# A row-wise softmax inside a fused attention and mixture-of-experts kernel: the row maximum is subtracted on TensorE instead of VectorE

## The chip, the cores and the metric

One core of one Trainium2 chip. The metric is the device time in microseconds (us) of one execution; times "of the span" are counted from its first instruction. Engines go by their short names: PE (TensorE, matrix products), PEld (its weight loads), DVE (VectorE), ACT (ScalarE), POOL (GpSimd), SP (SyncE, here only loads and stores).

## The reference

Sixteen tiles of 128 tokens and 128 features. Each token is normalised and attends among its own 16 heads: 16 x 16 scores per token, softmax over the last axis, weighted sum of the values, output projection, residual. Then a second normalisation, a router that sends each token to 2 of 8 experts, and the experts.

```
scores = jnp.einsum('blhk,blgk->blhg', Q_, K_) / jnp.sqrt(jnp.float32(D_K))
attn = jax.nn.softmax(scores, axis=-1)
x = jnp.einsum('blhg,blgv->blhv', attn, V_)
...
x = x + _L0_xattn_ref(_layernorm(x, axis=-1), ctx_1024, ctx_1024, ...)
x = x + _L0_ffn_ref(_layernorm(x, axis=-1), L0_ffn_router_w, ...)
```

The part that matters is the softmax of attn: exponential of (score minus its row's maximum), over rows of 16, 16 rows per token, so a tile has 128 partitions x 256 numbers.

## The kernel before, in words

Everything is f32. The program is written by hand: each engine has its own stream, semaphores join them, and the order on each engine is the order in which `step(g, j)` issues. A step number is s = 2 + j + 4g; in step s an engine works on several tiles at once: `tile_at(g, j, lag)` is tile s − lag. Steps of the middle groups run in a hardware loop. One tile t goes through this:

- ACT writes xn (L564, two steps ahead), PE turns it (L763), ACT copies it out as xnT (L604), PE projects it (L743) into bank 1 or 5.
- Step t, DVE: the product qk of the projection with the context, 128 x 2048 (L1021). PE then makes the score sum in bank 2 or 3: one product L772 and eight L775 of 256 columns each, with the identity as one operand.
- Step t + 1, DVE: the negated maximum of each row (L1034, neg_max), then the subtraction from the scores in PSUM into the SBUF tile shifted (L1043). ACT takes the exponential of shifted (L572) and writes probs. POOL multiplies probs with the context, 128 x 2048 (L310, called here POOL's product; for tile 15 DVE does it itself). probs and that product are the two parts of sums_in.
- Step t + 2, DVE (`normalised`): sums sums_in into z0, in the spare columns of bank 3 or 2 (L990), reciprocal, z (L1009). PE turns z (L788), ACT copies zT (L612), PE makes the output product with bias and residual (L794 to L796), ACT copies it to x_sb (L617).
- Step t + 3, DVE: the statistics of the new row (L994, L1003).

Every four tiles are a group. At tile 0 DVE also computes the first normalisation's shifts of groups 1 to 3 (`shifts`, L929 and L931, 128 x 4 each). At step s = 7 + 4n (NORM) POOL has made the power for group n's second normalisation (L473), right ahead of its product of the next tile; DVE makes shift2 of it (L1062, 128 x 4), and then sums z0. At s = 8 + 4n (LOGITS) ACT copies the turned rows xn2T (L636, `turned`), PE makes the router product (L755), and DVE the top experts (L1074 to L1086). At s = 9 + 4n (PLACES) the places are worked out and POOL begins to scatter rows (L511). After the last group DVE takes its product of tile 15, early_table and the router's steps; then come the experts, bound by PE, 39 tiles at 2.79 us.

Of the kernel before, what the change touches and what calls it, by code (L numbers as in the profile page):

```python
# [16 lines left out]
ALU = mybir.AluOpType  # L17
# [6 lines left out]
P = 128  # L24
NT = 16
G = 4
NG = NT // G
H = 16
# [23 lines left out]
def xattn_moe_kernel(nc, x, ctx, Wq, bq, Wk, bk, Wv, bv, Wo, bo, router_w, wv, sv, w, s, w1, s1, out):  # L52
    stack = ExitStack()
    with stack:
        def sb(name, shape, dt=F32):
            return stack.enter_context(nc.sbuf_tensor(name, shape, dt))
# [58 lines left out]
        shifted = sb("shifted", [P, 2, H, H])  # L115
# [145 lines left out]
        def quarter_of(j, lag):  # L261

            return (AHEAD + j - lag) % G

        def q_bank(b):

            return bank[1 + 4 * b]

        def z0_of(b):

            return bank[3 - b][:, H * H:H * H + P + H]
# [78 lines left out]
        with nc.Block() as block:  # L350
# [181 lines left out]
            def _(act):  # L532
# [23 lines left out]
                def step(g, j):  # L556
# [9 lines left out]

                    if a := tile_at(g, j, 1):
                        t, b = a
                        act.wait_ge(s_shifted, t + 1)
                        if second_on(t):  # L570
                            act.wait_ge(z0_ready, t - 1)
                        nc.scalar.activation(probs[:, b, :, :], shifted[:, b, :, :], ACT.Exp).then_inc(p_ready, 1)  # L572
# [13 lines left out]
                    if isinstance(g, int) and group_at(g, j, LOGITS) == (NG - 2,):  # L586
                        turned(NG - 2)
# [105 lines left out]
            def _(pe):  # L693
# [33 lines left out]

                def value_turned():

                    pe.wait_ge(setup_dve, 4)  # L730
                    nc.tensor.transpose(bank[7][:, 0:P], o_projT[:, :], ident[:, :])
                    nc.tensor.transpose(bank[7][0:HD, P:2 * P], out_biasT[:, :], ident[:, :]).then_inc(setup_pe, 1)

                def step(g, j):

                    if a := tile_at(g, j, -1):
                        t, b = a
                        pe.wait_ge(xnT_ready, t + 1)
                        if second_on(t):
                            pe.wait_ge(qk_ready, t - 1)  # L740
                        elif t == 0:
                            pe.wait_ge(setup_dve, 3)
                        nc.tensor.matmul(q_bank(b)[:, 0:P], xnT[:, quarter_of(j, -1), :],  # L743
                                         q_proj[:, 0:HD, :].rearrange("p i h -> p (i h)"),
                                         start=True, stop=True).then_inc(q_psum, 1)
# [21 lines left out]
                    if a := tile_at(g, j, 0):  # L767
                        t, b = a
                        pe.wait_ge(qk_ready, t + 1)
                        if second_on(t):  # L770
                            pe.wait_ge(s_shifted, t - 1)
                        nc.tensor.matmul(bank[2 + b][:, 0:H * H], xnT[:, quarter_of(j, 0), :],  # L772
                                         q_proj[:, HD, :].unsqueeze(2).to_broadcast([P, H, H]), start=True, stop=False)
                        for i in range(HD):
                            mm = nc.tensor.matmul(bank[2 + b][:, 0:H * H], ident[:, :], qk[:, b, i, :],  # L775
                                                  start=False, stop=(i == HD - 1))
                        mm.then_inc(s_psum, 1)
                    if (a := group_at(g, j, LOGITS)) and not isinstance(g, int):
                        places(a[0])
# [120 lines left out]
            def _(dve):  # L900
# [76 lines left out]
                def step(g, j):  # L977
# [48 lines left out]
                    if a := tile_at(g, j, 1):  # L1026
# [6 lines left out]
                        scores = bank[2 + b][:, 0:H * H].rearrange("p (h g) -> p h g", h=H)  # L1033
                        v.tensor_reduce(neg_max[:, b, :], scores, AX_X, ALU.max, negate=True).then_inc(max_ready, 1)  # L1034
# [3 lines left out]
                    if a := tile_at(g, j, 1):  # L1038
                        t, b = a
                        dve.wait_ge(max_ready, t + 1)  # L1040
                        if second_on(t):
                            dve.wait_ge(p_ready, t - 1)
                        v.tensor_tensor(shifted[:, b, :, :], scores,  # L1043
                                        neg_max[:, b, :].unsqueeze(2).to_broadcast([P, H, H]), ALU.add).then_inc(s_shifted, 1)
# [238 lines left out]
```

## Time and profile before

| | us |
|---|---|
| median of 3 runs | 294.7 |
| lowest, highest | 293.94, 297.12 |
| the profiled execution | 297.16 |
| its span | 295.4 |

The page lists the busy time of each engine, the share of the span in 40 slices of 7.4 us, the granted clock of PE in tenths of full speed (2.4 GHz; 5 is 1.2 GHz), and the chain of work that ended last. The timeline lists instructions in order of their start: start, duration, engine, line, operation, tiles, and in brackets how long the engine was idle before and what ended that. Each f32 product is two records of PE, so x16 is eight products.

### The profile page before, as it was taken

What the parts mean: (1) busy time and instruction counts of PE and PEld (TensorE: products, weight loads), DVE (VectorE), ACT (ScalarE), POOL (GpSimd) and SP (SyncE); (2) the same over time, 40 slices, a digit from 0 to 9 for tenths busy, and PEclk for the clock granted to TensorE, in tenths of its full rate; (3) what the DMA queues carried; (4) which work ended last, traced back from release to release, by engine and by line L of the source; (5) the groups of instructions that cost most, each with busy time, mean ns of one, the idle gap of its engine ahead of it and who ended that gap; (6) DMA issues with size and microseconds to landing.
All of it is one profiled execution on the core that took longest, in us unless ns stands there. A gap on an engine that the chain in (4) does not pass through costs nothing.

```text
span 295.4 us, 5940 instructions
## 1 busy us (share of the span) xinstructions
PE 246.9 (84%) x1587; PEld 220.5 (75%) x1588; DVE 208.5 (71%) x468; ACT 113.7 (38%) x281; POOL 164.8 (56%) x138
## 2 busy tenths in 40 slices
PE   7995988884998779899087999899999999999900
PEld 7884767662876668777065899899999999999800
DVE  3879899959999869894999477745555555555416
ACT  2421142324225354231225594445555555555200
POOL 7745569897356798669840477763323323323310
PEclk9988799998579996999655699999999999999965
DMA  5979980000000001000011213232111111000049
GB/s 151 280 207 407 265 330 2 3 1 0 0 3 0 18 9 36 9 0 18 18 36 37 61 51 103 82 109 76 43 48 41 45 50 53 27 18 24 9 149 278
DMA packets 22506, 22.88 MB, mean 77 GB/s; under 512 B 2717, under 2 KB 17985, under 8 KB 22355
## 3 DMA queue, kind: packets, MB, share of 16 engines
q1 hardware_dynamic: 18700, 17.30, 19.7%
q0 software_dynamic: 2528, 4.77, 4.9%
q10 hardware_dynamic: 1254, 0.55, 0.8%
q8 instruction: 10, 0.16, 0.2%
q14 instruction: 14, 0.11, 0.1%
HBM read 16.26 MB, written 6.80 MB: 78 GB/s over the span
## 4 chain that ended last, share of the span: by engine, by line
PE 53%; DVE 14%; issue 11%; POOL 10%; ACT 5%; DMA 4%; SPq 0%; ACTq 0%; POOLq 0%; DVEq 0%
PE bank L857 19%; PE bank L775 10%; PE bank L874 9%; POOL sums_in L310 5%; DVE shift L1062 3%; POOL routed L511 3%; PE bank L700 3%; DVE bank L990 2%; DMA sums_in<-expert_out 2%; DVE qk L1021 2%; PE bank L772 2%; PE bank L794 2%; POOL rstd L473 1%; PE bank L796 1%; PE bank L795 1%
## 5 line engine op out<-in xcount | busy, mean ns | idle before, releaser
L310 POOL TENSOR_TENSOR sums_in<-sums_in,ctx_ig 128x2048 f32<-128x2048 f32 x15 | 67.6, 4503 | 27.0 <-ACT sums_in L572 26.9
L525 POOL DMA_INDIRECT expert_out<-yo,xs x39 | 37.8, 970 | 56.5 <-DVE yo L1214 53.7
L775 PE MATMUL bank<-qk,ident 128*128 128x256 f32 x256 | 65.7, 416 | 0.0
L775 PEld LDWEIGHTS bank<-qk,ident 128*128 128x128 f32 x256 | 54.8, 214 | 9.4
L857 PE MATMUL bank<-xsT,g_tile 128*128 128x128 f32 x312 | 42.4, 280 | 0.6 <-issue 0.6
L857 PE MATMUL bank<-xsT,v_tile 128*128 128x128 f32 x312 | 41.6, 277 | 0.0
L874 PE MATMUL bank<-w_sb,ctx_sb 128*128 x312 | 41.4, 276 | 0.0
L990 DVE TENSOR_REDUCE bank<-sums_in 128x144 f32<-128x2304 f32 x16 | 40.8, 2552 | 0.1
L1204 DVE TENSOR_TENSOR ctx_sb<-bank,ctx_sb 128x512 f32<-128x512 f32 x39 | 26.9, 690 | 18.2 <-PE bank L857 17.8
L511 POOL DMA_INDIRECT routed<-rows,pos x32 | 31.7, 990 | 14.3 <-issue 13.0
L857 PEld LDWEIGHTS bank<-xsT,g_tile 128*128 128x128 f32 x312 | 38.8, 195 | 0.9 <-ACT g_tile L665 0.8
L857 PEld LDWEIGHTS bank<-xsT,v_tile 128*128 128x128 f32 x312 | 38.4, 194 | 0.0
L874 PEld LDWEIGHTS bank<-w_sb,ctx_sb 128*128 128x128 f32 x312 | 38.0, 192 | 0.2 <-issue 0.2
L1021 DVE TENSOR_TENSOR qk<-bank,ctx_ig 128x2048 f32<-128x2048 f32 x16 | 36.5, 2286 | 0.9 <-issue 0.6
L673 ACT ACTIVATE ctx_sb<-bank 128x512 f32<-128x512 f32 x39 | 23.3, 598 | 24.9 <-PE bank L857 24.3
L1197 DVE COPY v_tile<-v_sb 128x512 f32 x39 | 17.2, 441 | 19.1 <-issue 18.3
L665 ACT COPY g_tile<-g_sb 128x512 f32 x39 | 24.1, 617 | 12.6 <-PE bank L857 12.3
L1214 DVE SCALAR_TENSOR_TENSOR yo<-bank,xs,wo_sb 128x128 f32<-128x128 f32 x39 | 13.7, 350 | 12.2 <-PE bank L874 11.0
L612 ACT COPY zT<-bank 128x128 f32<-128x128 f32 x16 | 4.2, 265 | 40.8 <-PE bank L788 40.8
L1062 DVE SCALAR_TENSOR_TENSOR shift<-mv,rstd 128x4 f32<-128x4 f32 x4 | 9.2, 2308 | 9.8 <-POOL rstd L473 9.8
L667 ACT COPY xsT<-bank 128x128 f32<-128x128 f32 x39 | 10.3, 265 | 13.9 <-PE bank L844 13.8
L788 PE MATMUL bank<-ident,z 128*128 128x128 f32 x16 | 5.3, 330 | 12.2 <-DVE z L1009 12.2
(163 smaller groups left out, 325.7 us busy)
## 6 DMA issues: line engine op xcount, KB each, us to landing
xs<-routed SPq DMA_DIRECT2D x39, 65.0 KB, 1.9
g_sb<-in_L_ffn_w_dram SPq DMA_DIRECT2D x1, 2048.0 KB, 11.8
g_scale<-in_L_ffn_s_dram SPq DMA_DIRECT2D x1, 2048.0 KB, 16.3
v_sb<-in_L_ffn_wv_dram SPq DMA_DIRECT2D x1, 2048.0 KB, 26.8
sums_in<-expert_out SPq DMA_DIRECT2D x3, 512.0 KB, 4.8
x_sb<-in_x_dram SPq DMA_DIRECT2D x4, 256.0 KB, 6.0
ctx_sb<-in_ctx_dram SPq DMA_DIRECT2D x4, 256.0 KB, 6.3
out_dram<-x_sb SPq DMA_DIRECT2D x3, 256.0 KB, 2.9
```

The source lines that it names most:

```text
L310: return eng.tensor_tensor(pv[:, b, :, :].rearrange("p (h i) g -> p h i g", h=H), probs[:, b, :, :].unsqueeze(2).to_broadcast([P, H, HD, H ...
L511: pool.indirect_dma_start(out=routed[:, :], out_offset=bass.IndirectOffsetOnAxis(ap=pos[:, m % TOP, m // TOP:m // TOP + 1], axis=0), in_=r ...
L525: pool.indirect_dma_start(out=expert_out[:, :], out_offset=bass.IndirectOffsetOnAxis(ap=xs_i[:, t % XB, P:P + 1], axis=0), in_=yo[:, t % X ...
L665: nc.scalar.copy(g_tile[:, c % 2, :], g_sb[:, bass.ds(at, F)]).then_inc(g_tile_ready, 1)
L673: nc.scalar.activation(act_sb[:, c % 2, :], bank[1 + c % 2][:, :], ACT.Gelu_apprx_tanh).then_inc(act_ready, 1)
L775: mm = nc.tensor.matmul(bank[2 + b][:, 0:H * H], ident[:, :], qk[:, b, i, :], start=False, stop=(i == HD - 1))
L857: mm = nc.tensor.matmul(psum[:, n * P:n * P + P], weights[:, c % 2, n * P:n * P + P], xsT[:, c % 2, :], start=True, stop=True)
L874: mm = nc.tensor.matmul(bank[5 + c % 2][:, 0:P], hid[:, c % 2, n * P:n * P + P], w1_sb[:, bass.ds(y_at + n * P, P)], start=(n == 0), stop= ...
L990: v.tensor_reduce(z0_of(b), sums_in[:, b, :, :], AX_X, ALU.add).then_inc(z0_ready, 1)
L1021: v.tensor_tensor(qk[:, b, :, :].rearrange("p i (h g) -> p i h g", h=H), q_bank(b)[:, 0:P].rearrange("p (i h) -> p i h", i=HD).unsqueeze(3 ...
L1062: v.scalar_tensor_tensor(shift2[:, :], mv2[:, :, 0], -1.0, rstd2[:, :], ALU.mult, ALU.mult).then_inc(shift2_ready, 1)
L1204: v.tensor_tensor(hid[:, c % 2, :], bank[3 + c % 2][:, :], act_sb[:, c % 2, :], ALU.mult).then_inc(hid_ready, 1)
```

## The change

The subtraction leaves DVE, and the tile shifted goes. PE adds the negated maximum to the scores of tile t, where they stand in PSUM, by a product of the identity with neg_max (each entry repeated over its row). That product, `minus_max`, is issued inside the score sum of tile t + 1, after two of its eight products (MAX_AFTER = 1); for the last tile by itself. It waits for max_ready and increments s_shifted. ACT takes the exponential from the bank. z0 moves from the score banks to the spare columns of the projection banks 1 and 5, with a wait of the projection for z_ready. The score sum waits for p_ready where it waited for s_shifted; the maximum of t waits for s_shifted of t − 2. For group 2, ACT's copy of xn2T (`turned`) moves ahead of the exponential.

```diff
--- before.py
+++ after.py
@@ -112,7 +112,6 @@
         xnT = sb("xnT", [P, G, P])
         qk = sb("qk", [P, 2, HD, H * H])
         neg_max = sb("neg_max", [P, 2, H])
-        shifted = sb("shifted", [P, 2, H, H])
         sums_in = sb("sums_in", [P, 2, P + H, H])
         rowinv = sb("rowinv", [P, 2, H])
         pv, probs = sums_in[:, :, 0:P, :], sums_in[:, :, P:P + H, :]
@@ -268,7 +267,7 @@
 
         def z0_of(b):
 
-            return bank[3 - b][:, H * H:H * H + P + H]
+            return bank[1 + 4 * b][:, P:P + P + H]
 
         def group_at(g, j, lag):
 
@@ -564,12 +563,15 @@
                         nc.scalar.activation(xn[:, b, :], x_sb[:, t, :], ACT.Identity, scale=rstd[:, bass.ds(t, 1)],
                                              bias=shift[:, bass.ds(t, 1)]).then_inc(xn_ready, 1)
 
+                    if isinstance(g, int) and group_at(g, j, LOGITS) == (NG - 2,):
+                        turned(NG - 2)
                     if a := tile_at(g, j, 1):
                         t, b = a
                         act.wait_ge(s_shifted, t + 1)
                         if second_on(t):
                             act.wait_ge(z0_ready, t - 1)
-                        nc.scalar.activation(probs[:, b, :, :], shifted[:, b, :, :], ACT.Exp).then_inc(p_ready, 1)
+                        nc.scalar.activation(probs[:, b, :, :], bank[2 + b][:, 0:H * H].rearrange("p (h g) -> p h g", h=H),
+                                             ACT.Exp).then_inc(p_ready, 1)
                     for n, turns in enumerate(((-1, 0), (-1, 3), (0, 0), (0, 1))):
                         if isinstance(g, int) and (g, j) == turns:
                             turn(n)
@@ -583,8 +585,6 @@
                             t = n * G + m
                             nc.scalar.activation(xn2[:, m, :], x_sb[:, t, :], ACT.Identity, scale=rstd2[:, m:m + 1],
                                                  bias=shift2[:, m:m + 1]).then_inc(xn2_ready, 1)
-                    if isinstance(g, int) and group_at(g, j, LOGITS) == (NG - 2,):
-                        turned(NG - 2)
                     if (a := group_at(g, j, LOGITS)) and not isinstance(g, int):
                         logits_exponentials(a[0])
 
@@ -725,6 +725,17 @@
                                               start=True, stop=True)
                     mm.then_inc(setup_pe, 1)
 
+                MAX_AFTER = 1
+
+                def minus_max(g, j):
+
+                    if a := tile_at(g, j, 1):
+                        t, b = a
+                        pe.wait_ge(max_ready, t + 1)
+                        nc.tensor.matmul(bank[2 + b][:, 0:H * H], ident[:, :],
+                                         neg_max[:, b, :].unsqueeze(2).to_broadcast([P, H, H]),
+                                         start=False, stop=True, skip_group_check=True).then_inc(s_shifted, 1)
+
                 def value_turned():
 
                     pe.wait_ge(setup_dve, 4)
@@ -740,6 +751,8 @@
                             pe.wait_ge(qk_ready, t - 1)
                         elif t == 0:
                             pe.wait_ge(setup_dve, 3)
+                        if not isinstance(t, int) or t >= G:
+                            pe.wait_ge(z_ready, t - (G - 1))
                         nc.tensor.matmul(q_bank(b)[:, 0:P], xnT[:, quarter_of(j, -1), :],
                                          q_proj[:, 0:HD, :].rearrange("p i h -> p (i h)"),
                                          start=True, stop=True).then_inc(q_psum, 1)
@@ -768,13 +781,17 @@
                         t, b = a
                         pe.wait_ge(qk_ready, t + 1)
                         if second_on(t):
-                            pe.wait_ge(s_shifted, t - 1)
+                            pe.wait_ge(p_ready, t - 1)
                         nc.tensor.matmul(bank[2 + b][:, 0:H * H], xnT[:, quarter_of(j, 0), :],
                                          q_proj[:, HD, :].unsqueeze(2).to_broadcast([P, H, H]), start=True, stop=False)
                         for i in range(HD):
                             mm = nc.tensor.matmul(bank[2 + b][:, 0:H * H], ident[:, :], qk[:, b, i, :],
                                                   start=False, stop=(i == HD - 1))
+                            if i == MAX_AFTER:
+                                minus_max(g, j)
                         mm.then_inc(s_psum, 1)
+                    else:
+                        minus_max(g, j)
                     if (a := group_at(g, j, LOGITS)) and not isinstance(g, int):
                         places(a[0])
                     if a := tile_at(g, j, 2):
@@ -1031,17 +1048,14 @@
                                 statistics(n)
                         dve.wait_ge(s_psum, t + 1)
                         scores = bank[2 + b][:, 0:H * H].rearrange("p (h g) -> p h g", h=H)
+                        if second_on(t):
+                            dve.wait_ge(s_shifted, t - 1)
                         v.tensor_reduce(neg_max[:, b, :], scores, AX_X, ALU.max, negate=True).then_inc(max_ready, 1)
                     elif not group_at(g, j, NORM):
                         normalised()
 
                     if a := tile_at(g, j, 1):
                         t, b = a
-                        dve.wait_ge(max_ready, t + 1)
-                        if second_on(t):
-                            dve.wait_ge(p_ready, t - 1)
-                        v.tensor_tensor(shifted[:, b, :, :], scores,
-                                        neg_max[:, b, :].unsqueeze(2).to_broadcast([P, H, H]), ALU.add).then_inc(s_shifted, 1)
                         if isinstance(t, int) and t == 0:
                             for n in range(1, NG):
                                 shifts(n)
```

What the order of instructions is before and after, at three places. PE, one quiet step in the middle of the attention stage, from the projection to the turning of z (before):

```order
L743 MATMUL bank<-q_proj,xnT 128x128
L760 REGISTER_ALU
L763 MATMUL bank<-ident,xn 128x128
L772 MATMUL bank<-q_proj,xnT 128x256
L775 MATMUL bank<-qk,ident 128x256 x8
L788 MATMUL bank<-ident,z 128x128
L794 MATMUL bank<-o_proj,zT 128x128
```

and the same step of the changed kernel:

```order
L756 MATMUL bank<-q_proj,xnT 128x128
L773 REGISTER_ALU
L776 MATMUL bank<-ident,xn 128x128
L785 MATMUL bank<-q_proj,xnT 128x256
L788 MATMUL bank<-qk,ident 128x256 x2
L735 MATMUL bank<-neg_max,ident 128x256
L788 MATMUL bank<-qk,ident 128x256 x6
L805 MATMUL bank<-ident,z 128x128
```

L735 is new; it belongs to the tile before the one whose sum stands around it.

DVE at tile 0, from its maximum over the shifts of groups 1 to 3 to the next product qk (before):

```order
L1034 TENSOR_REDUCE neg_max<-bank 128x16
L1043 TENSOR_TENSOR shifted<-bank,neg_max 128x256
L929 SCALAR_TENSOR_TENSOR shift<-mv,rstd 128x4
L931 TENSOR_SCALAR shift<-shift 128x4
L929 SCALAR_TENSOR_TENSOR shift<-mv,rstd 128x4
L931 TENSOR_SCALAR shift<-shift 128x4
L929 SCALAR_TENSOR_TENSOR shift<-mv,rstd 128x4
L931 TENSOR_SCALAR shift<-shift 128x4
L1021 TENSOR_TENSOR qk<-bank,ctx_ig 128x2048
```

and changed:

```order
L1053 TENSOR_REDUCE neg_max<-bank 128x16
L946 SCALAR_TENSOR_TENSOR shift<-mv,rstd 128x4
L948 TENSOR_SCALAR shift<-shift 128x4
L946 SCALAR_TENSOR_TENSOR shift<-mv,rstd 128x4
L948 TENSOR_SCALAR shift<-shift 128x4
L946 SCALAR_TENSOR_TENSOR shift<-mv,rstd 128x4
L948 TENSOR_SCALAR shift<-shift 128x4
L1038 TENSOR_TENSOR qk<-bank,ctx_ig 128x2048
```

The subtraction is gone and the six small instructions follow the maximum directly.

PE at the end of the attention stage, from the last score sum (tile 15) on, first before:

```order
L775 MATMUL bank<-qk,ident 128x256 x8
L788 MATMUL bank<-ident,z 128x128
L794 MATMUL bank<-o_proj,zT 128x128
L795 MATMUL bank<-out_bias,ones 128x128
L796 MATMUL bank<-x_sb,ident 128x128
L802 MATMUL bank<-ident,xn 128x128 x4
L755 MATMUL bank<-router,xn2T 128x8 x4
L788 MATMUL bank<-ident,z 128x128
```

then changed, from the turning of tile 13's z:

```order
L805 MATMUL bank<-ident,z 128x128
L811 MATMUL bank<-o_proj,zT 128x128
L812 MATMUL bank<-out_bias,ones 128x128
L813 MATMUL bank<-x_sb,ident 128x128
L819 MATMUL bank<-ident,xn 128x128 x4
L768 MATMUL bank<-router,xn2T 128x8 x4
L735 MATMUL bank<-neg_max,ident 128x256
L805 MATMUL bank<-ident,z 128x128
```

The product that tile 15's exponential waits for stands behind the router product of group 2.

## Rows read from the trace of the kernel before

**Rows 1.** The page: busy times, the granted clock in slices, the chain by engine.

```profile
PE 246.9 (84%) x1587; PEld 220.5 (75%) x1588; DVE 208.5 (71%) x468; ACT 113.7 (38%) x281; POOL 164.8 (56%) x138
...
PEclk9988799998579996999655699999999999999965
...
PE 53%; DVE 14%; issue 11%; POOL 10%; ACT 5%; DMA 4%; SPq 0%; ACTq 0%; POOLq 0%; DVEq 0%
```

**Rows 2.** Timeline, tile 0 to tile 3: PE, DVE, POOL (start, duration, engine, line).

```profile
19.51 0.60 PE L772 MATMUL bank<-q_proj,xnT 128*128 128x256 f32 x2
37.52 0.60 PE L772 MATMUL bank<-q_proj,xnT 128*128 128x256 f32 x2
...
20.68 0.17 DVE L931 TENSOR_SCALAR shift<-shift 128x4 f32<-128x4 f32 x1
20.96 4.42 DVE L931 TENSOR_SCALAR shift<-shift 128x4 f32<-128x4 f32 x1
28.77 2.54 DVE L990 TENSOR_REDUCE bank<-sums_in 128x144 f32<-128x2304 f32 x1
...
20.85 4.50 POOL L310 TENSOR_TENSOR sums_in<-sums_in,ctx_ig 128x2048 f32<-128x2048 f32 x1 [1.83 <-ACT sums_in L572]
```

**Rows 3.** Timeline, one quiet round: DVE, PE, POOL.

```profile
41.62 0.42 DVE L1034 TENSOR_REDUCE neg_max<-bank 128x16 f32<-128x256 f32 x1 [0.53 <-PE bank L775]
44.28 0.60 PE L772 MATMUL bank<-q_proj,xnT 128*128 128x256 f32 x2
44.44 4.50 POOL L310 TENSOR_TENSOR sums_in<-sums_in,ctx_ig 128x2048 f32<-128x2048 f32 x1 [2.23 <-ACT sums_in L572]
44.72 3.62 PE L775 MATMUL bank<-qk,ident 128*128 128x256 f32 x16
```

**Rows 4.** Groups by line and form: total busy us, mean ns of one, idle before.

```profile
L1043 DVE TENSOR_TENSOR shifted<-bank,neg_max 128x256 f32<-128x256 f32 x16 | 6.8, 424 | 0.6
L572 ACT ACTIVATE sums_in<-shifted 128x256 f32<-128x256 f32 x16 | 6.5, 408 | 11.6 <-DVE shifted L1043 11.6
```

**Rows 5.** Timeline, tiles 5 to 8 with group 0's second normalisation: POOL, DVE, PE.

```profile
58.30 4.53 POOL L310 TENSOR_TENSOR sums_in<-sums_in,ctx_ig 128x2048 f32<-128x2048 f32 x1 [1.23 <-ACT sums_in L572]
65.27 4.50 POOL L310 TENSOR_TENSOR sums_in<-sums_in,ctx_ig 128x2048 f32<-128x2048 f32 x1
...
65.33 4.45 DVE L1062 SCALAR_TENSOR_TENSOR shift<-mv,rstd 128x4 f32<-128x4 f32 x1 [2.22 <-POOL rstd L473]
...
65.06 0.60 PE L772 MATMUL bank<-q_proj,xnT 128*128 128x256 f32 x2
73.11 0.47 PE L788 MATMUL bank<-ident,z 128*128 128x128 f32 x1 [4.00 <-DVE z L1009]
79.69 1.06 PE L772 MATMUL bank<-q_proj,xnT 128*128 128x256 f32 x2
```

**Rows 6.** Timeline, tiles 13 to 15 with group 2's second normalisation: PE, POOL, DVE.

```profile
124.61 0.61 PE L772 MATMUL bank<-q_proj,xnT 128*128 128x256 f32 x2
136.32 0.68 PE L772 MATMUL bank<-q_proj,xnT 128*128 128x256 f32 x2
...
138.77 1.04 POOL L473 TENSOR_TENSOR rstd<-vtmp,minus_half 128x4 f32<-128x4 f32 x1
139.80 4.47 POOL L310 TENSOR_TENSOR sums_in<-sums_in,ctx_ig 128x2048 f32<-128x2048 f32 x1
...
139.84 4.45 DVE L1062 SCALAR_TENSOR_TENSOR shift<-mv,rstd 128x4 f32<-128x4 f32 x1 [3.11 <-POOL rstd L473]
```

**Rows 7.** Timeline, the end of the attention stage: PE, DVE.

```profile
147.62 0.47 PE L788 MATMUL bank<-ident,z 128*128 128x128 f32 x1 [7.16 <-DVE z L1009]
152.22 1.88 PE L755 MATMUL bank<-router,xn2T 128*128 128x8 f32 x8 [0.68 <-ACT xn2T L636]
...
151.72 2.28 DVE L310 TENSOR_TENSOR sums_in<-sums_in,ctx_ig 128x2048 f32<-128x2048 f32 x1
```

**Rows 8.** Windows: length, busy of PE, PEld, DVE, ACT, POOL, granted clock.

```profile
143.40:167.30 23.90, 16.17 (x60) 12.96 (x61) 19.09 (x63) 9.34 (x25) 8.42 (x10) 0.51 0.15 40
```

## The prediction

> **What bounds the kernel now.** I read the page's busy shares first, then its chain, then the timeline of each engine through the attention stage. The shares [rows 1] name nobody: PE is busy 84% of the span, DVE 71%, POOL 56%. The chain gives 53% to PE, and most of that is the expert stage after 192 us, which the change does not touch. So the time is decided by how early the attention stage hands over. There is one number for that: DVE's own product of tile 15 starts at 151.72 [rows 7], and from it 295.4 − 151.7 = 143.7 us follow in code that is the same in both kernels. I ask only when that product starts.
>
> In a quiet round [rows 3] tile follows tile every 6.76 us (L772 at 37.52 [rows 2] and at 44.28). PE and ACT make that round, one waiting for the other: score sum, turn z, output product, copy, next xn, turn it. DVE is not the limit there: it waits 0.53 us for the score sum before each maximum. POOL's product takes 4.50 of the 6.76.
>
> What breaks the quiet are DVE instructions that take 4.4 us instead of 0.16: L931 at 20.96 (its sister at 20.68 took 0.17) [rows 2], L1062 at 65.33 [rows 5] and again at 139.84 [rows 6]. Each began 0.04 to 0.11 us after a POOL product L310 and ended with it. So a small DVE instruction on SBUF that comes just behind a POOL product loses the whole product. After the second and third PE had nothing to do for 4.00 and 7.16 us (the waits in its rows at 73.11 [rows 5] and 147.62 [rows 7]) and then ran at 1.2 GHz: the clock line of the page is 5 and 7 there, and the stretch 143.4 to 167.3 has a granted clock of 0.51 [rows 1, 8].
>
> The Trainium skill has this as a rule (SBUF — State Buffer, "SBUF: two separate sides"): DVE and GpSimd share a port pair under an exclusive lock, the first to start holds it for its whole instruction. By the rule a DVE instruction that came first would delay the product by only 0.16 us; no row shows that case. It is rival A below.
>
> **The change, part by part.**
>
> 1. DVE loses the subtraction: 16 × 0.42 = 6.8 us [rows 4]. In the quiet round this is worth nothing by itself, since DVE waits for PE there.
>
> 2. PE gains one product of 256 columns per tile. From the start of L772 at 44.28 to that of L775 at 44.72 [rows 3] one such product takes 0.44. It sits in PE's ring, so each quiet round becomes 6.76 + 0.44 = 7.20.
>
> 3. The exponential of tile t, and with it POOL's product of t, now waits for the score sum of t+1: L772, two partial products, the new one, 4 × 0.44 = 1.76, then 0.2 for the drain, 0.41 for the exponential [rows 4] and 0.1 of signalling: 2.45 after L772 starts. Before, the product started 0.16 after L772 (44.44 against 44.28). So each product starts 2.3 us later in its round. Product and DVE's sum over it still fit: 2.45 + 4.50 + 3.2 (z0, reciprocal, z) = 10.2, and z is wanted at 7.20 + 4.4 = 11.6 by the next score sum's end. Behind the waiting exponential on ACT stand the copies of xnT and zT, wanted 2 us later or more.
> The Trainium skill (VectorE: DVE Perf Modes, the section on the TRN2 errata) gives a ScalarE instruction 224 cycles plus its elements when it reads SBUF and 172 when it reads PSUM. The row has 408 ns for the exponential from SBUF, the rule 400, so they agree there. By it the new exponential is 0.04 us shorter; were all 16 on the path, the total would be 0.7 lower. No row has this exponential from PSUM; I count it as 0.41.
>
> 4. Tile 0. The product cannot start until 19.51 + 2.45 = 21.96, instead of 20.85. DVE's last small shift instruction, which began at 20.96, moves up by the 0.42 of the subtraction to 20.54 and is over at 20.7, so the stall of 4.25 goes. What is late next is the product: it ends at 26.5, DVE's sum starts at 26.6 instead of 28.77 and z is ready at 29.7. PE, which was kept from tile 2's score sum until 27.6 and then ran it at 1.2 GHz, has it done by about 29. From z to the next L772 the ring takes 6.76 − 3.9 = 2.86. Tile 3's L772: 32.6 instead of 37.52, **4.9 earlier**.
>
> 5. Tiles 3 to 7: four rounds at 0.44 more. Tile 7's L772 at 65.06 − 4.9 + 1.8 = 62.0 [rows 5], **3.1 earlier**.
>
> 6. Group 0's statistics. POOL's product of tile 5 started at 58.30 and the one of tile 6 at 65.27, directly behind the scaling and the power: 6.97. Tile 6's L772 now comes one round of 7.20 before tile 7's, at 54.8; product 5 starts at 54.8 + 2.45 = 57.25, so the power is done at 64.2. Exponential 6 is done at 62.0 + 2.4 = 64.4. DVE's L1062 wins by 0.2 and the stall of 4.3 goes. z of tile 5 comes before PE is idle long, and the clock stays at 2.4 GHz. From z to tile 8's L772 took 6.6 us at the low clock (73.11 to 79.69); of this I estimate 2 to 2.6 as the clock's (most of the PE work in it at twice its quick time). Lead at tile 8: 3.1 + 4.3 = 7.4 at least; I take **7.4**, since the product of tile 7 (2.3 later in its round) now limits.
>
> 7. Tiles 8 to 13: five rounds at 0.44 take 2.2 back, and the two router steps, where the product starts later than before behind the new wait, another 1.2 or so. Lead at tile 13's L772 (124.61 [rows 6]): between 2.5 and 5.2; I take **4.0**.
>
> 8. Group 2's statistics, counted from that L772. Before: power done at 15.20, product 14 at 15.19, L1062 blocked. Now: the power is 0.44 later, because two scatters ahead of product 13 wait for a copy behind one longer score sum: 15.6. Tile 15's L772 was at 11.71 and comes at 12.6; exponential 14 is done 2.4 later, at 15.0. That is 0.6 before POOL is free, so the product again starts at once and L1062 stalls as before. z of tile 13 comes **0.4 later** counted from there.
>
> 9. The end. Before, DVE took its product of tile 15 as soon as z of tile 14 was written: 151.72, 4.10 after PE began to turn z of tile 13 (147.62) [rows 7]. Now it needs exponential 15, whose product stands on PE behind the four router products (152.22 to 153.95 at the low clock), and these behind ACT's copy of xn2T. The new product takes 0.85 at 1.2 GHz, then 0.24 and 0.5: the exponential is done at 155.55, which is 7.9 after the turn began. **3.8 later.** At 2.4 GHz I estimate the same chain at 5.2 and the loss at 1.1.
>
> Sum: −4.0 + 0.4 + 3.8 = +0.2. The span becomes 295.6 and the profiled execution 297.4. That execution is the slowest of the ones shown, whose median is 294.7. With 0.1 for rounding up I forecast 295.0: no change that a measurement of this kernel can tell (about 1%). Its own range is 293 to 297.
>
> **The rivals.**
>
> A. Group 2's instruction wins. For it: the margin is 0.6 us after 15, and a slower PE in tiles 14 and 15 would close it. Against it: the margin has the wrong sign in the sum. It gives back 4.3, and PE idles shorter before the end, so that the loss there is between 1.1 and 3.8, say 1.2 less: 295.0 − 5.5 = 289.5. Chance 0.22.
>
> B. The saving on DVE is what counts: 6.8 off, 288. Against it the wait of 0.53 us [rows 3] in every quiet round. Chance 0.06.
>
> C. Slower: group 0's instruction loses. The place is L1062 of group 0, the price 4.3, and it decides when exponential 6 is done before the power on POOL; I have 0.2 us between them. Then POOL's product starts directly, and the lead at tile 8 is 3.1 instead of 7.4: 299.3. Chance 0.14.
>
> D. Slower by the clock: PE now waits elsewhere (z of tile 7 or 11 behind a later product) and falls to 1.2 GHz for one more score sum. Nine products at 0.85 instead of 0.44 are 3.7 us: 298.5. Against it: PE has more columns to stream in each round than before. Chance 0.13.
>
> The forecast itself has 0.45. Of it 0.02 lies below the 1% bound and 0.03 above it. Faster by over 1%: 0.22 + 0.06 + 0.02 = 0.30; slower by over 1%: 0.27 + 0.03 = 0.30; within 1%: 0.40. The range reaches to rival A and to rival C: 289.5 to 299.5.
>
> **What would show it.** Right: L310 of POOL starts about 2.4 us after each score sum's first product; no small shift instruction over 1 us at tile 0; L1062 of groups 0, 1, 2 at 0.16, 0.16 and over 4 us; tile 3's first score product at 32 to 33 us; DVE's product of tile 15 at 151 to 153, ended by a wait for ACT. Wrong: L1062 of group 2 short (then A), that of group 0 long (then C), a clock of 5 in the slices between 88 and 110 us (then D), quiet rounds under 6.7 us (then B). If DVE's product of tile 15 starts on time and the total is still another, what I left out lies in the expert stage.

## The result, and the profile of the changed kernel

The changed kernel takes 298.38 us in the median (298.07 to 300.45, 4 runs) against 294.44 us: ratio 1.0143, 95% interval [1.0099, 1.0188]. It is slower by 1.4%. The forecast was 295.0, the range 289.5 to 299.5, and slower by over 1% had a chance of 0.3. The profiled execution took 298.07, with a span of 296.2. Ratios compare fast runs alone, while the medians given beside some of them are of all runs of a kernel, slow ones too.

The page of the changed kernel, the lines that answer to [rows 1]:

```profile
PE 250.9 (85%) x1619; PEld 224.6 (76%) x1620; DVE 194.0 (65%) x452; ACT 113.7 (38%) x281; POOL 165.1 (56%) x138
...
PEclk9999799997977989799655599999999999999975
...
PE 66%; POOL 9%; DVE 7%; ACT 6%; issue 5%; DMA 4%; ACTq 1%; SPq 0%; POOLq 0%; DVEq 0%
```

DVE is 14.5 us less busy and PE 4.0 more, and the chain has moved from DVE (14% to 7%) to PE (53% to 66%). The span is 0.8 us longer all the same: the work taken from DVE was not what the end waited for.

The timeline, first of DVE: the six shift instructions, shift2 of groups 0, 1 and 2, then tile 14's z and the product of tile 15. The lines of POOL are its products of tiles 0, 6 and 14:

```profile
19.10 0.17 DVE L948 TENSOR_SCALAR shift<-shift 128x4 f32<-128x4 f32 x1
63.44 0.16 DVE L1076 SCALAR_TENSOR_TENSOR shift<-mv,rstd 128x4 f32<-128x4 f32 x1 [4.12 <-POOL rstd L472]
100.15 0.16 DVE L1076 SCALAR_TENSOR_TENSOR shift<-mv,rstd 128x4 f32<-128x4 f32 x1 [2.80 <-POOL rstd L472]
136.02 4.45 DVE L1076 SCALAR_TENSOR_TENSOR shift<-mv,rstd 128x4 f32<-128x4 f32 x1 [2.70 <-POOL rstd L472]
147.69 0.29 DVE L1026 TENSOR_TENSOR z<-bank,rowinv 128x128 f32<-128x128 f32 x1
151.78 2.29 DVE L309 TENSOR_TENSOR sums_in<-sums_in,ctx_ig 128x2048 f32<-128x2048 f32 x1 [3.80 <-ACT sums_in L573]
...
20.14 4.52 POOL L309 TENSOR_TENSOR sums_in<-sums_in,ctx_ig 128x2048 f32<-128x2048 f32 x1 [1.27 <-ACT sums_in L573]
63.78 4.51 POOL L309 TENSOR_TENSOR sums_in<-sums_in,ctx_ig 128x2048 f32<-128x2048 f32 x1 [0.38 <-ACT sums_in L573]
135.98 4.47 POOL L309 TENSOR_TENSOR sums_in<-sums_in,ctx_ig 128x2048 f32<-128x2048 f32 x1
```

The stalls at tile 0 and at group 0 are gone [rows 2, 5]. In group 0 shift2 starts 0.34 us ahead of the product. The stall of group 2 has stayed as in [rows 6]: there the small instruction is 0.04 behind. At the end DVE has z at 147.98 and then waits 3.80 us for the exponential of tile 15.

PE in a quiet round, then the first products of the score sums of tiles 1, 3, 13 and 15, then the end:

```profile
39.31 0.60 PE L785 MATMUL bank<-q_proj,xnT 128*128 128x256 f32 x2
39.75 1.03 PE L788 MATMUL bank<-qk,ident 128*128 128x256 f32 x4
40.61 0.59 PE L735 MATMUL bank<-neg_max,ident 128*128 128x256 f32 x2
41.04 2.75 PE L788 MATMUL bank<-qk,ident 128*128 128x256 f32 x12
46.33 0.33 PE L776 MATMUL bank<-ident,xn 128*128 128x128 f32 x1 [0.52 <-ACT xn L563]
46.49 0.60 PE L785 MATMUL bank<-q_proj,xnT 128*128 128x256 f32 x2
...
17.68 0.60 PE L785 MATMUL bank<-q_proj,xnT 128*128 128x256 f32 x2
31.06 1.06 PE L785 MATMUL bank<-q_proj,xnT 128*128 128x256 f32 x2
118.70 1.06 PE L785 MATMUL bank<-q_proj,xnT 128*128 128x256 f32 x2
132.92 0.68 PE L785 MATMUL bank<-q_proj,xnT 128*128 128x256 f32 x2
143.80 0.48 PE L805 MATMUL bank<-ident,z 128*128 128x128 f32 x1 [6.31 <-DVE z L1026]
148.40 1.88 PE L768 MATMUL bank<-router,xn2T 128*128 128x8 f32 x8 [0.68 <-ACT xn2T L636]
150.13 1.20 PE L735 MATMUL bank<-neg_max,ident 128*128 128x256 f32 x2
```

The round is 46.49 − 39.31 = 7.18 us, where it was 6.76. From the start of the new product in it to that of the next, 40.61 to 41.04, is 0.43 (forecast 0.44). The last rows are the new end: the subtraction of tile 15 stands behind the router product, at 1.2 GHz.

So against the profile of before the attention stage ends when it was forecast to, though not by all of the forecast's terms (see below). The turn of tile 13's z is 3.8 us earlier (143.80 against 147.62 [rows 7]), the end gives 3.9 back, and DVE's product of tile 15 starts at 151.78 against 151.72. The whole span is then 0.8 longer, 0.7 of it behind that product. Yet the medians lie 3.9 apart. The question for the runs is twofold: are the terms real, and where are the other 3 us?

### The profile page after: what moved, and what is told of

Same layout as the page of the kernel before. It is cut to its first block, busy times and chain, and to the rows that moved or that the text cites. A ratio compares the mean times of both kernels' runs of the same rounds, so it can differ in the third digit from the quotient of the medians.

```text
span 296.2 us, 5990 instructions
## 1 busy us (share of the span) xinstructions
PE 250.9 (85%) x1619; PEld 224.6 (76%) x1620; DVE 194.0 (65%) x452; ACT 113.7 (38%) x281; POOL 165.1 (56%) x138
## 4 chain that ended last, share of the span: by engine, by line
PE 66%; POOL 9%; DVE 7%; ACT 6%; issue 5%; DMA 4%; ACTq 1%; SPq 0%; POOLq 0%; DVEq 0%
PE bank L874 21%; PE bank L788 11%; PE bank L891 10%; POOL sums_in L309 5%; POOL routed L510 3%; PE bank L700 3%; PE bank L785 3%; PE bank L735 2%; PE bank L811 2%; PE bank L813 2%; PE bank L812 2%; DMA sums_in<-expert_out 2%; DVE bank L1007 2%; PE bank L768 2%; DVE shift L1076 2%
## 5 line engine op out<-in xcount | busy, mean ns | idle before, releaser
L788 PEld LDWEIGHTS bank<-qk,ident 128*128 128x128 f32 x256 | 52.7, 206 | 8.4
L665 ACT COPY g_tile<-g_sb 128x512 f32 x39 | 24.1, 617 | 12.6 <-PE bank L874 12.3
L573 ACT ACTIVATE sums_in<-bank 128x256 f32<-128x256 f32 x16 | 6.1, 384 | 48.4 <-PE bank L735 48.4
L667 ACT COPY xsT<-bank 128x128 f32<-128x128 f32 x39 | 10.3, 265 | 14.8 <-PE bank L861 14.5
L811 PE MATMUL bank<-o_proj,zT 128*128 128x128 f32 x32 | 8.7, 359 | 6.7 <-ACT zT L612 6.7
L617 ACT COPY x_sb<-bank 128x128 f32<-128x128 f32 (+1 forms) x16 | 4.3, 266 | 26.1 <-PE bank L813 26.1
```

The costliest lines, as they stand in the source:

```text
L665: nc.scalar.copy(g_tile[:, c % 2, :], g_sb[:, bass.ds(at, F)]).then_inc(g_tile_ready, 1)
```

## The experiments

Twelve kernels ran, in three sets of four. In the first two sets all kernels took some 18 to 20 us longer than in the third, the kernel before too (314.5 and 315.6 against 296.1). In the profile of before the extra lies behind 172 us, in gaps in which ACT and DVE waited for something that the trace does not name. Ratios are taken against the runs of before in the same set, and times within the attention stage are compared across.

**The changed kernel without its end.** The last minus_max goes ahead of tile 13's output product on PE, and the exponential of tile 15 right behind the copy of zT on ACT:

```diff
 # PE, behind the turn of z of tile 13
+if (g, j) == (NG - 1, 1):
+    minus_max(NG - 1, 2)
 # ACT, behind the copy of zT of tile 13
+if (g, j) == (NG - 1, 1):
+    exponential(NG - 1, 2)
```

> Changed kernel with the last minus_max (tile 15) issued on PE directly behind the turn of tile 13's z, and its exponential on ACT directly behind the copy of zT, ahead of the router product. Theory 1: DVE's product of tile 15 starts at 148.0 to 148.5 us instead of 151.78, the time falls by 3.4 to 3.8 us to 294.7 +- 0.7, ratio to before 1.00. Rival: what follows is set by the router product and tile 14's output, not by that product: under 1 us off, ratio 1.010 to 1.014.

Ratio 1.0016 [0.9974, 1.0058]. DVE at its end, timeline:

```profile
147.90 0.29 DVE L1035 TENSOR_TENSOR z<-bank,rowinv 128x128 f32<-128x128 f32 x1
148.11 2.28 DVE L309 TENSOR_TENSOR sums_in<-sums_in,ctx_ig 128x2048 f32<-128x2048 f32 x1
```

The product starts as soon as z is written, at 148.11, 3.7 us earlier. Without this one term the change is even with the kernel before: the end is worth 0.9 to 1.3% (against 1.0105 and 1.0143), 2.8 to 4 us. The rival falls.

**The small instruction first.** POOL's products wait for the shifts; in the kernel before:

```diff
 pool.wait_ge(p_ready, t + 1)
 ...
+if t == 0:
+    pool.wait_ge(ln1_shift, NG)
+if group_at(g, j, NORM):
+    pool.wait_ge(shift2_ready, n + 1)
 values(pool, t, b).then_inc(pv_ready, 1)
```

> Kernel before, but POOL's product of tile 0 also waits for the shifts of groups 1 to 3, and its products of tiles 6, 10, 14 for shift2 of their group, so that the small DVE instruction goes first. Theory 1 (the lost product is a matter of who starts first): L931 and L1062 take 0.2 us everywhere, POOL's product starts 0.2 to 0.3 us later, and the time falls by 3 us for tile 0, by 4.3 plus about 2 of low clock each for groups 0 and 2, less what rings give back: 282 to 287 us. Rival (something else slows these instructions, or the next wait is as late): under 2 us off, above 292.

Ratio 0.9675 [0.9622, 0.9728], from three of its six runs; the medians of all its runs and of all those of before, 306.6 against 314.5, give 0.975. Timeline of DVE and POOL at tile 0 and group 0, and DVE's product of tile 15:

```profile
19.20 0.17 DVE L935 TENSOR_SCALAR shift<-shift 128x4 f32<-128x4 f32 x1
59.73 0.16 DVE L1066 SCALAR_TENSOR_TENSOR shift<-mv,rstd 128x4 f32<-128x4 f32 x1 [2.22 <-POOL rstd L473]
137.34 2.28 DVE L310 TENSOR_TENSOR sums_in<-sums_in,ctx_ig 128x2048 f32<-128x2048 f32 x1
...
19.54 4.54 POOL L310 TENSOR_TENSOR sums_in<-sums_in,ctx_ig 128x2048 f32<-128x2048 f32 x1 [0.61 <-DVE shift L935]
60.07 4.52 POOL L310 TENSOR_TENSOR sums_in<-sums_in,ctx_ig 128x2048 f32<-128x2048 f32 x1 [0.36 <-DVE shift L1066]
```

The product waits 0.36 us and takes no longer for it, and the small instruction takes 0.16. So which of the two starts first decides whether 0.4 or 4.4 us are lost. The end of the attention stage is 14.4 us earlier than in [rows 7]; 7.9 us (2.5%, by the medians) to 10.2 us (3.25%, by the ratio) of it shows in the times.

The three waits one at a time, in the kernel before (tile 0, group 0, group 2):

> Kernel before with the wait at tile 0 alone (POOL's product of tile 0 behind the six shift instructions). Theory 1 (all three stalls of the profile are in the ordinary executions too, each a loser): L931 short, about 1.5% faster (0.98 to 0.99), since the lead of 7 us of the profile is given back in part at the later stalls. Theory 2 (ordinary executions of before already win one of the three races; the profile, which has all three, is 2.7 to 6 us above them): where it is this one, ratio 0.995 to 1.005.

> Kernel before with the wait at group 0 alone (product of tile 6 behind shift2). In before's profile the two started 0.06 us apart. Theory 1: 1.5% faster (4.3 us). Theory 2, where it is this race that ordinary executions win: 0.995 to 1.005 while its profile is 4 us or more below before's profile.

> Kernel before with the wait at group 2 alone (product of tile 14 behind shift2); in before's profile 0.04 us apart. Theory 1: 1.5 to 2% faster. Theory 2, where it is this race that ordinary executions win: 0.995 to 1.005.

Ratios 0.9919 [0.9877, 0.9960], 0.9906 [0.9860, 0.9952] and 0.9919 [0.9878, 0.9960]. By these each stall is worth 0.8 to 0.9%; by the medians of all runs (313.88, 312.65 and 314.09 against 315.55) it is 0.5 to 0.9%. That is 1.5 to 3 us, less than the 4.3 that it lasts. No ratio is at 1.00, so no race is shown that ordinary executions always win, though two of the medians give 0.995, the edge of theory 2; 1.5% for each, theory 1, was too much. The profiles show where a gain goes: in each of the three another small instruction of group 1 is caught that was free in the profile behind the prediction, picked for 5.01 us at 114.28 and for 5.00 at 108.80, gates for 4.28 at 120.84. In the first of them, a long execution of 318.25 us, DVE's product of tile 15 starts at 151.93, no earlier than in [rows 7]. What the changed kernel gets for nothing, the first two stalls, is 1.4 to 1.75% together, 4.5 to 5.5 us.

**The same wait in the changed kernel:**

> The same wait in the changed kernel, where only group 2's L1076 was still blocked (4.45 us at 136.02). Theory 1: it takes 0.16, z of tile 13 is written 4.2 us earlier, PE idles 2 us instead of 6.3, the low clock costs less: 4.2 to 6 us off, 292.4 to 294.2 us. Rival: exponential 15 or POOL's product of 14 takes over and under 2 us are gained: above 296.4.

Ratio 0.9938 [0.9897, 0.9979]. Timeline of POOL and DVE:

```profile
135.93 0.16 DVE L1080 SCALAR_TENSOR_TENSOR shift<-mv,rstd 128x4 f32<-128x4 f32 x1 [2.70 <-POOL rstd L472]
145.92 2.29 DVE L309 TENSOR_TENSOR sums_in<-sums_in,ctx_ig 128x2048 f32<-128x2048 f32 x1 [1.90 <-ACT sums_in L577]
...
136.26 4.49 POOL L309 TENSOR_TENSOR sums_in<-sums_in,ctx_ig 128x2048 f32<-128x2048 f32 x1 [0.36 <-DVE shift L1080]
```

The product of tile 15 starts 5.9 us earlier than in the changed kernel's first profile, and its wait falls from 3.80 to 1.90. Taken off 1.0105 and 1.0143, the ratio gives 1.7 to 2.0%, 5.2 to 6.4 us. This is rival A's price: worked out as 5.5.

**Both, and minus_max at another place.** First the two edits together, then also minus_max ahead of the turn of the next xn:

```diff
 # PE's step
+minus_max(g, j)
 if a := tile_at(g, j, -2):        # the turn of xn
     pe.wait_ge(xn_ready, t + 1)
 ...
-            if i == MAX_AFTER:
-                minus_max(g, j)
```

> Changed kernel with both the wait of POOL's products for the shifts and the last minus_max and exponential moved ahead. Alone they gave about 1.7% and 1.0%. If they add: 0.982 to 0.988 of before. If the shorter idle time of PE already gave back most of the end's loss (product of tile 15 waited 1.90 us instead of 3.80): 0.986 to 0.992.

> As a_yield_tail, with minus_max issued ahead of PE's turn of the next xn, where PE waits 0.3 to 1.1 us for ACT, instead of inside the score sum. Theory 1 (the product's 0.44 us per tile is on PE's ring): quiet rounds 6.8 instead of 7.2, POOL's product starts before the next score sum, 3 to 5 us off: 0.970 to 0.980 of before. Rival (the ring is ACT's or the product fits beside other waits only in part): rounds stay at 7.1 to 7.2, within 0.4% of a_yield_tail.

Ratios 0.9895 [0.9818, 0.9973] and 0.9762 [0.9698, 0.9826]. Whether the first two edits add isn't settled: the interval takes in both expectations. In the trace the product of tile 15 starts at 145.18 against 145.92 with the wait alone, though PE turned tile 13's z 1.25 us later (140.67 against 139.42). Counted from that turn, the new end saves 2.0 us: the 1.90 that DVE still waited, and not 3.8. The third edit gives 1.3% more, and its six executions (287.65 to 289.31) all lie below the shortest with two edits (291.26). PE in a quiet round of the last kernel:

```profile
37.45 0.61 PE L798 MATMUL bank<-q_proj,xnT 128*128 128x256 f32 x2
...
43.35 0.60 PE L746 MATMUL bank<-neg_max,ident 128*128 128x256 f32 x2
44.04 0.33 PE L789 MATMUL bank<-ident,xn 128*128 128x128 f32 x1
44.20 0.61 PE L798 MATMUL bank<-q_proj,xnT 128*128 128x256 f32 x2
```

The round is 44.20 − 37.45 = 6.75, as before the change: the product fills the 0.52 us in which PE waited for xn. At its place inside the sum it cost the whole 0.43. POOL's product comes earlier with it too, 0.24 us behind the score sum's first product (37.69 against 37.45) where it was 2.4, so the 1.3% is the price of the late place as a whole. Of all kernels run, the one before with POOL's waits has the lowest ratio (0.9675), and this one the second (0.9762). They ran in different sets, their intervals overlap, and the medians of all runs give 0.975 for both (here 288.67 against 296.08), so which of the two is quicker isn't shown.

**The missing 3 us.** Both kernels once more, unchanged:

> The kernel before, once more, for a second profile. Theory 1: its ordinary execution (294.4 us) is 2 to 3 us shorter than the profiled one (297.1) because it loses one stall or one stretch of low clock less in the attention stage, so DVE's product of tile 15 starts at 148 to 150 us in a profile at 294 us, against 151.72. Rival: the difference lies in the expert stage, and that product starts at 151 to 152 again. Ratio to before 1.00 in both.

> The changed kernel once more. Theory 1 and 2 alike: ratio to before 1.010 to 1.019 as measured first. Theory 2 adds: its profiled execution lies within 0.5% of its median (no race of it is near: 0.34 us between L1076 and the product of tile 6, 0.6 us before the product of tile 14).

The changed kernel repeats: ratio 1.0105 [1.0050, 1.0161], product of tile 15 at 151.6, and its profiled execution (317.59) lies 0.2% from its median, as theory 2 had it. The kernel before gave 1.0014 [0.9971, 1.0057] against itself, and its profile again has all three stalls and again lies high, at 321.1 where its median is 314.8, with a granted clock of 0.852 where most of its other executions have 0.88. Two rows of DVE and two of POOL in its timeline:

```profile
117.25 5.08 DVE L1086 TENSOR_TENSOR picked<-pick 128x32 f32<-128x32 f32 x1 [0.49 <-DVE pick L1082]
155.08 2.28 DVE L310 TENSOR_TENSOR sums_in<-sums_in,ctx_ig 128x2048 f32<-128x2048 f32 x1
...
116.78 0.97 POOL L511 DMA_INDIRECT routed<-rows,pos  x1 [0.30 <-issue]
117.78 4.49 POOL L310 TENSOR_TENSOR sums_in<-sums_in,ctx_ig 128x2048 f32<-128x2048 f32 x1
```

Here one more small instruction is caught, picked of group 1. It began 0.53 us ahead of POOL's product of tile 12, but inside POOL's scatter L511, and ended with the product: so to start before the product is not enough where POOL goes from a scatter straight into it. In the first profile the same instruction took 0.22:

```profile
116.82 0.22 DVE L1086 TENSOR_TENSOR picked<-pick 128x32 f32<-128x32 f32 x1
```

(Both profiles of before have yet another, which the prediction doesn't list: L1077, 128x8, 2.76 us at 80.17 in the first.) Tile 15's product then starts 3.4 us later than in [rows 7]. So the kernel before carries its spread in itself: some tenths of a microsecond decide which small instructions are caught, and its two profiles differ in that. This profile too is of a long execution, so theory 1's 148 to 150 was not seen in it, and the rival's 151 to 152 neither.

Then I made the kernel before lose its races for certain, by two small memsets of a spare PSUM column on DVE between the wait for the power and shift2, in groups 0 and 1, and in another kernel in group 2:

```diff
 dve.wait_ge(rstd2_ready, n + 1)
+v.memset(bank[7][:, 400:416], 0.0).then_inc(late_step, 1)
+dve.wait_ge(late_step, ...)
+v.memset(bank[7][:, 400:416], 0.0).then_inc(late_step, 1)
+dve.wait_ge(late_step, ...)
 v.scalar_tensor_tensor(shift2[:, :], ...)
```

> Kernel before with two small memsets of a spare PSUM column on DVE between the wait for the power and shift2 of groups 0 and 1, so that in group 0 the small instruction starts 0.2 us later and surely behind POOL's product of tile 6. Question: do ordinary (not profiled) executions of before win this race, which its profile loses? Theory 2a (they win it, and this is why the profiled execution is 6 us above the median): ratio to before 1.010 to 1.018. Theory 3 (they lose it as the profile shows; the profiled execution is longer by granted clock alone): 0.998 to 1.004.

> The same two memsets at group 2 alone, against POOL's product of tile 14. Theory 2b (ordinary executions win the race at group 2): 1.010 to 1.018. Theory 3: 0.998 to 1.004.

Ratios 1.0042 [0.9981, 1.0102] and 0.9991 [0.9941, 1.0042]. At group 2 this fits theory 3: ordinary executions lose that race too, as the profile shows. At group 0 the interval takes in both theories, and it stays open: by the medians of all runs it is 298.45 against 296.08 (1.008), and five of the twelve executions (299.3 to 301.0) are longer than all of before's but one, of 595 us. That edit is in group 1 too, where picked is caught for 5.22 us at 114.50 in its profile, so the loss can't be put down to group 0.

The executions of before in this set fall into bunches: 7 of 22 at 293.6 to 293.9 us (clock 0.902), 6 at 295.0 to 296.2, and 9 at 297.3 to 297.7, three of which have a clock of 0.886. The profile that the prediction rests on, 297.16 us at 0.887, has the time and clock of these three. Of the shorter bunches no profile of the unchanged kernel was taken. The nearest is that of the kernel made to lose group 2 (295.82 us at 0.905). PE in its timeline at tiles 0 and 1, and DVE's product of tile 15:

```profile
13.44 0.60 PE L773 MATMUL bank<-q_proj,xnT 128*128 128x256 f32 x2
17.66 0.60 PE L773 MATMUL bank<-q_proj,xnT 128*128 128x256 f32 x2
...
150.00 2.28 DVE L311 TENSOR_TENSOR sums_in<-sums_in,ctx_ig 128x2048 f32<-128x2048 f32 x1
```

Here, and in both profiles of the changed kernel, the score sum of tile 0 runs at 2.4 GHz. In the profile of before tile 1's score sum starts at 19.51 [rows 2], 1.85 us later, since the clock was at 1.2 GHz for part of the stretch ahead of it (granted clock 0.76, first row below). Windows of the two kernels, first before, columns as in [rows 8]:

```profile
12.00:19.00 7.00, 7.00 (x34) 6.14 (x34) 5.44 (x20) 0.66 (x2) 3.36 (x5) 0.76 0.71 155
89.00:96.00 7.00, 6.03 (x31) 4.81 (x31) 6.51 (x14) 3.69 (x12) 4.53 (x1) 1.00 0.00 0
119.00:126.00 7.00, 6.03 (x35) 5.07 (x34) 5.53 (x18) 2.53 (x10) 4.53 (x2) 0.99 0.00 0
```

and the changed kernel:

```profile
12.00:19.00 7.00, 7.00 (x43) 6.38 (x43) 6.32 (x26) 0.66 (x2) 3.41 (x5) 1.00 0.72 165
89.00:96.00 7.00, 5.87 (x21) 4.73 (x21) 5.52 (x7) 2.56 (x9) 4.49 (x4) 0.76 0.06 19
119.00:126.00 7.00, 6.61 (x25) 5.21 (x24) 4.96 (x8) 3.00 (x10) 3.30 (x1) 0.79 0.00 0
```

Where the early low stretch is missing, DVE of the kernel before, with two memsets more, starts tile 15's product at 150.0 us, with the group 2 stall in it. The changed kernel's 151.78 is 1.8 more, and its span 2.2 more (296.2 against 294.0), of the 3.9 between the medians. That ordinary short executions of the kernel before lack that stretch is argued from this one profile and not shown. Nor is it shown that the change has no part in it: the stretch is in four of the eight profiles of before and its variants and in none of the six of the changed kernel and its own.

## Why the prediction was right or wrong

- **Parts 1 and 2, the round.** Right. DVE's saving is worth nothing in a quiet round, and PE's ring went from 6.76 to 7.18 (forecast 7.20). Moving the same product into PE's wait gives the 0.4 back, so it was the place and not the product that cost.
- **Part 3, the product's start.** Right in the quiet rounds: 2.46 us behind the score sum's first product at tile 0 (20.14 against 17.68; forecast 2.45). In eight of the fifteen tiles, where a scatter or the power on POOL or a stretch of low clock comes in between, it was 3.1 to 4.1. The exponential from PSUM takes 384 ns where it took 408 from SBUF [rows 4]. The rule of the Trainium skill (VectorE: DVE Perf Modes, the section on the TRN2 errata) gave 0.04 less, the rows 0.02.
- **Parts 4 and 6, two stalls gone.** Right in place and sign. Tile 3's score sum starts 6.5 us earlier (31.06 against 37.52), of which 1.8 is the clock of tile 0; the rest, 4.6, answers to the 4.9. Group 0's small instruction won by 0.34, forecast 0.2. A fourth stall of before, L1077 for 2.76 us at 80.17, isn't in the forecast, and is gone as well (slot_of is caught for 1.2 us at 78.55 instead).
- **Parts 5, 7 and 8, the lead.** Forecast 4.0 us at tile 13 and 3.1 at tile 15 (0.9 lost between them); measured 5.9 (118.70 against 124.61) and 3.4 (132.92 against 136.32). Of both, 1.8 came from the clock of tile 0, which no term of the forecast holds. Without it the lead is 4.1 at tile 13, as forecast, and 1.6 at tile 15. Between them PE ran the first of tile 13's products at 1.2 GHz: its first record takes 1.06 us where it took 0.61 [rows 6], the granted clock is 0.79 from 119 to 126 us, and the two tiles take 14.2 us, forecast 12.6. In the second profile of the changed kernel, where tile 13's sum has the full clock (120.17, 0.60 us), they take the forecast 12.6, but tile 13 itself is 1.5 us later. Each profile has lost about 1.5 of the forecast lead by tile 15, at different places. This is rival D in a small form. Of its sign, a clock of 5 between 88 and 110 us, half came: 0.76 in the window of 89 to 96, which stands in all five profiles with the new product inside the score sum, and not in the one with it ahead of the turn of xn. But two variants of before have such a stretch within 94 to 100 us, so that the later product causes it is argued and not shown. Tile 3's sum began at the low clock too (31.06, 1.06 us).
- **Part 8, group 2 stalls again.** Right: 4.45 us at 136.02. Forced in the kernel before, the same loss changes nothing (0.9991), so it is the usual case there.
- **Part 9, the end.** Right: DVE waits 3.80 us (forecast 3.8 later), and the kernel without this term is even with before (1.0016).
- **The most likely outcome, no change, did not come.** What missed it is the last step: "That execution is the slowest of the ones shown, whose median is 294.7." I took 2.4 us off 297.4 as if the changed kernel had the same long execution. It doesn't: its profile (298.07) is its shortest of four runs. The 2.4 were part of the kernel before's own spread, in which its profiled execution is one of the long ones, with an early stretch of low clock. So the base of the comparison was wrong by 2.4.
- **Luck.** Profile against profile the forecast was 297.4 and the measured time 298.07, 0.7 off. That is closer than the working earned: 1.8 us that the clock of tile 0 gave made up for 1.5 that later stretches of low clock took. Put against the profile without the early stretch (150.0), the product of tile 15 came 1.8 later, where the sum had 0.2. And the range held 298.38 by the width that rivals C and D gave it. Neither came about as written.
- **Rivals.** A did not occur by itself; made to occur it gave 5.2 to 6.4 us (worked out 5.5). B is refuted by the round. C did not occur. D in part; its own price of 3.7 on 295.0 is 298.7, not 298.5.

In ratios: two stalls gone give 1.75% back (1.4% by medians). The end costs 0.9 to 1.3%, the place inside the score sum 1.3%. That leaves 0.5 to 0.9% slower where 1.05 to 1.43% was measured; each term is uncertain by about 0.5%, so the rest can't be assigned.

## What to carry to other kernels

Work moved off an engine that waits in every round gains nothing, and the engine that takes it pays in full unless the work is put into one of that engine's own waits. Where a long POOL instruction and a small DVE one of a kind that it holds (next section) are released at the same moment, let the long one wait for the small one: here that gave 2.5 to 3.25%, as much as the best version of the change, which has this wait too. Before a forecast is anchored on a profiled execution, look at where it lies among the other executions: its distance from the median is a property of that execution, and does not carry over to the changed kernel.

## What the runs showed of the hardware

POOL's product holds only some of DVE's small instructions on SBUF, fewer than the prediction's words say. The kernel made to lose group 0, timeline of DVE and POOL:

```profile
61.88 0.07 DVE L1066 MEMSET bank<- 128x16 f32 x1
61.99 4.13 DVE L1068 SCALAR_TENSOR_TENSOR shift<-mv,rstd 128x4 f32<-128x4 f32 x1
...
61.62 4.47 POOL L311 TENSOR_TENSOR sums_in<-sums_in,ctx_ig 128x2048 f32<-128x2048 f32 x1
```

The memset of PSUM took 0.07 us inside the product, and the next instruction 4.13, to the product's end. The kernel before, in the product of 90.41:

```profile
92.25 0.18 DVE L1003 BATCH_NORM_AGGREGATE mv<-stats 128x2 f32<-128x6 f32 x1
92.28 0.06 DVE L1002 MEMSET pause_dve<- 128x1 f32 x1
...
90.41 4.53 POOL L310 TENSOR_TENSOR sums_in<-sums_in,ctx_ig 128x2048 f32<-128x2048 f32 x1 [5.05 <-ACT sums_in L572]
```

Both work on SBUF alone, and neither is held. In the fourteen profiles the aggregate mv stands inside a product 101 times and takes 0.17 to 0.18 us each time. Held were those that combine two SBUF operands (shift from mv and rstd, r, picked, slot_of, carry, gates), and the tensor-scalar of shift, which has one. Apart from one carry that began 0.03 us behind the product's start and took 0.13, each of them lasted to the product's end or past it. Where a second product followed at once, slot_of was held through both: 7.26 us at 110.34 in the kernel with minus_max ahead of the turn.

And the loser of such a race need not be a known one: where group 2 was made to lose, the carry of group 1 met a product of POOL and took 4.46 us at 118.71 (0.13 in the first profile of before). That others are caught in their place, as here and in the three kernels with one wait, is the likely reason why removing one stall is worth less than the 4.3 us that it lasts; it wasn't tested by itself.
